# The end of a softmax attention: last scores in five accumulator banks, and the next norm begun ahead of the barrier

## What is computed

```python
def _layernorm(x, axis=-1, eps=1e-05):
    m = jnp.mean(x, axis=axis, keepdims=True)
    v = jnp.var(x, axis=axis, keepdims=True)
    return (x - m) / jnp.sqrt(v + eps)

# layer 1, attention: x is (2, 1024, 128), 16 heads of 8 features
scores = jnp.einsum('bhsd,bhed->bhse', q, k) * scale
attn = jax.nn.softmax(scores, axis=-1)
out = jnp.einsum('bhse,bhed->bhsd', attn, v)
...
return out @ Wo.T + bo          # added to the residual stream

# layer 1, experts: top 1 of 8, x is the normalised residual stream
router_logits = x @ Wr.T
expert_idx = jnp.argmax(jax.nn.softmax(router_logits, axis=-1), axis=-1)
```

## Time and profile before

| | |
|---|---|
| three timed runs | 938.89, 940.71, 941.74 us; median 940.71 |
| profiled execution | 944.2 us, its span 942.9 us |
| busy in the span | TensorE 757.7, VectorE 669.1, ScalarE 509.2, GpSimd 244.2 us |
| attention 1 | about 450 to 820.7 us |
| experts 1 | 820.7 us to the end |

### The profile page before, as it was taken

The page is one execution under the profiler, slowest core; times in us unless marked ns, Lnnn a source line. Parts: engine busy times, 40 slices in busy tenths (PEclk is TensorE's granted clock), DMA queues, the critical chain, the costliest instruction groups (busy, mean ns, idle before and its releaser), DMA issues. The chain is left out here.

```text
span 942.9 us, 17693 instructions
## 1 busy us (share of the span) xinstructions
PE 757.7 (80%) x6704; PEld 324.7 (34%) x6704; DVE 669.1 (71%) x1321; ACT 509.2 (54%) x1003; POOL 244.2 (26%) x297
## 2 busy tenths in 40 slices
PE   6879987976419999937887999999999999628780
PEld 3332245633316676624111222222222222215560
DVE  7879944467673434448786999999999998553545
ACT  4723522555304333343346888888888888404343
POOL 0130010323045666560651200000100000025653
PEclk9989999988659999977658999999999999858996
DMA  3520010000541111131876030321300000051112
GB/s 92 127 54 2 1 24 5 5 1 0 231 158 37 44 43 42 38 100 51 230 158 188 2 80 2 80 47 36 80 2 2 3 2 12 16 235 42 42 34 95
DMA packets 40618, 57.62 MB, mean 61 GB/s; under 512 B 12424, under 2 KB 27920, under 8 KB 39768
## 3 DMA queue, kind: packets, MB, share of 16 engines
q1 hardware_dynamic: 36568, 48.36, 18.9%
q0 software_dynamic: 3968, 8.13, 3.0%
HBM read 37.54 MB, written 14.75 MB: 55 GB/s over the span
## 5 line engine op out<-in xcount | busy, mean ns | idle before, releaser
L983 DVE TENSOR_REDUCE arena<-psum 128x1 f32<-128x1024 f32 x256 | 300.9, 1217 | 23.9 <-PE psum L877 21.2
L1113 ACT ACTIVATE arena<-psum 128x512 f32<-128x512 f32 x512 | 266.8, 604 | 57.2 <-PE psum L894 57.2
L877 PE MATMUL psum<-arena 56*128 56x512 bf16 x512 | 180.8, 413 | 10.9 <-DVE arena L983 9.2
L894 PE MATMUL psum<-arena 59*128 59x512 bf16 x512 | 157.8, 390 | 8.1 <-ACT arena L1113 6.1
L905 PE MATMUL psum<-arena 128*32 128x512 f32 x1024 | 138.1, 611 | 8.7 <-issue 8.7
L894 PEld LDWEIGHTS psum<-arena 59*128 59x128 bf16 x512 | 38.3, 94 | 172.2 <-ACT arena L1113 148.8
L473 POOL DMA_INDIRECT rows_y<-arena x62 | 61.7, 996 | 62.7 <-DVE arena L424 59.7
L381 PEld LDWEIGHTS psum<-arena 128*128 128x128 f32 x496 | 62.3, 191 | 39.2 <-issue 29.7
L381 PE MATMUL psum<-arena 128*128 (+1 forms) x496 | 66.8, 278 | 10.7 <-ACT arena L452 10.4
L372 PE MATMUL psum<-arena 128*128 x124 | 67.5, 627 | 3.0 <-DVE arena L409 2.6
L468 POOL DMA_INDIRECT arena<-rows_x,arena x62 | 60.3, 972 | 35.3 <-issue 16.9
(11 more groups left out here) (305 smaller groups left out, 1111.8 us busy)
## 6 DMA issues: line engine op xcount, KB each, us to landing
arena<-scr_k SPq DMA_DIRECT2D x15, 448.0 KB
arena<-scr_q SPq DMA_DIRECT2D x15, 448.0 KB
arena<-in_f_up SPq DMA_DIRECT2D x1, 4096.0 KB, 13.7
arena<-rows_y SPq DMA_DIRECT2D x12, 256.0 KB, 4.8
scr_q<-arena SPq DMA_DIRECT2D x6, 384.0 KB, 3.7
arena<-in_f_down SPq DMA_DIRECT2D x1, 2048.0 KB, 19.8
rows_x<-xn SPq DMA_DIRECT2D x2, 1024.0 KB, 16.6
arena<-in_f_up SPq DMA_DIRECT2D x1, 2048.0 KB, 8.6
```

What stands on the lines that cost most here:

```text
L877: mm = pe.matmul(ps[:, bank + half, :], q[rows, k, h, (qh * 4 + qt) * P:(qh * 4 + qt + 1) * P], kk[rows, k, h, half * BLK:(half + 1) * BLK ...
L894: pe.matmul(ps[:, n % 3, :], kk[0:KA, k, h, kb * P:(kb + 1) * P], q[0:KA, k, h, qh * BLK:(qh + 1) * BLK], start=True, stop=True).then_inc( ...
L983: dve.tensor_reduce(mx[:, qh, h * 4 + qt:h * 4 + qt + 1], ps[:, bank:bank + 2, :].rearrange("p a b -> p (a b)"), X, ALU.max).then_inc(S("a ...
L1113: act.activation(pt[:, (u % 3) * HG + h, :], ps[:, n % 3, :], ACT.Exp, scale=float(HD) ** -0.5).then_inc(S("a1_exp"), 1)
```

## The change

The edits, by what they do.

1. **Five banks.** From score 464 on (the first of unit 116) the scores go through banks 5, 6 and the three old ones in turn. A score waits for the last exponential that read its bank, and the first in banks 5 and 6 for all 256 row maxima. `project_out(2)` and `project_out(3)`, whose banks are 5 and 6, wait for the last exponential that reads them.
2. **The norm of blocks 0 to 2 ahead of the barrier.** VectorE takes the variance plus epsilon of 12 tiles after `add_out(2)`, their reciprocals and an offset (mean x -1 x reciprocal) after `turn_back(3)`, and the four rows of block 0; ScalarE takes the root and, as one activation each with scale and offset, the eight rows of blocks 1 and 2; TensorE transposes the three blocks behind `project_out(3)`, in banks 0 to 2; ScalarE copies them to `xnT`.
3. **Behind the barrier** only block 3 is left: 4 columns of roots, 4 rows, 4 transposes, one copy. SyncE's `rows_out_sp` of this stage waits for a row count of 8 in place of 16 (the rows that ScalarE makes are not in that count).
4. `retire` leaves the semaphores with `_landed` and `_stored` in their names alone (eight of the `f0_` stage).

```diff
-def rows_out_sp(c, name, k):
-    c.sp.wait_ge(c.sem("n_row"), NT * (c.turn + 1))
+def rows_out_sp(c, name, k, rows=NT):
+    c.sp.wait_ge(c.sem("n_row"), NT * c.turn + rows)
...
-    rows_out_sp(c, "f1", 1)
+    rows_out_sp(c, "f1", 1, 2 * TPB)
...
 def ffn1_dve(c, x):
-    norm_roots(c, 1e-5)
-    for n in range(NB):
-        norm_rows(c, x, n)
+    last = slice(3 * TPB, NT)
+    dve.wait_ge(own.sem, own.n)
+    dve.tensor_scalar(m["rs"][:, last], m["mv"][:, last, 1], 1e-5, None, ALU.add).then_inc(S("n_var"), 1)
+    dve.wait_ge(S("n_root"), c.turn + 1)
+    dve_step(c, dve.reciprocal(m["rs"][:, last], m["rs"][:, last]))
+    norm_rows(c, x, 3)
...
 def ffn1_act(c):
-    norm_act(c, (6, 7), xnt_block(c))
+    act.wait_ge(S("n_var"), c.turn + 1)
+    act.activation(rs[:, 3 * TPB:NT], rs[:, 3 * TPB:NT], ACT.Sqrt).then_inc(S("n_root"), 1)
+    act.wait_ge(S("n_turned"), NB * (c.turn + 1))
+    act.copy(xnt_block(c)(3), c.psum[:, 6, :]).then_inc(S("n_xnt"), 1)
...
 def ffn1_pe(c):
-    norm_pe(c, (6, 7))
+    c.pe.wait_ge(c.sem("n_row"), NT * c.turn + 2 * TPB)
+    for j in range(TPB):
+        mm = c.pe.transpose(c.psum[:, 6, j * P:(j + 1) * P], c.mem["xn"][:, 3 * TPB + j, :], c.mem["ident"][:])
+    mm.then_inc(c.sem("n_turned"), 1)
...
+LAST_MAXIMA = (TILES - AHEAD + 1) // 2 + 1
+def score_bank(n):
+    first = LAST_MAXIMA * HG
+    return n % 3 if n < first else ((5, 6) + tuple((first + k) % 3 for k in range(3)))[(n - first) % 5]
+def score_ahead(n):
+    return max((k for k in range(max(0, n - 5), n) if score_bank(k) == score_bank(n)), default=None)
...
-        if n >= 3:
-            pe.wait_ge(S("a1_exp"), n - 2)
-        pe.matmul(ps[:, n % 3, :], kk[0:KA, k, h, kb * P:(kb + 1) * P],
+        if score_ahead(n) is not None:
+            pe.wait_ge(S("a1_exp"), score_ahead(n) + 1)
+        elif n >= LAST_MAXIMA * HG:
+            pe.wait_ge(S("a1_red"), TILES)
+        pe.matmul(ps[:, score_bank(n), :], kk[0:KA, k, h, kb * P:(kb + 1) * P],
...
     def project_out(b):
         pe.wait_ge(S("a1_back"), b + 1)
+        pe.wait_ge(S("a1_exp"), max((n + 1 for n in range(LAST_MAXIMA * HG, G * U * HG) if score_bank(n) == 3 + b), default=1))
...
     project_out(3)
+    for b in range(3):
+        pe.wait_ge(S("n_row"), NT * (c.turn + 1) + TPB)
+        if b:
+            pe.wait_ge(S("a1_nrow"), TPB * b)
+        for j in range(TPB):
+            mm = pe.transpose(ps[:, b, j * P:(j + 1) * P], c.mem["xn"][:, b * TPB + j, :], m["ident"][:])
+        mm.then_inc(S("n_turned"), 1)
...
     turn_back(2)
     add_out(2)
+    mv, rs, most = c.mem["mv"], c.mem["rs"], slice(0, 3 * TPB)
+    dve.wait_ge(own.sem, own.n)
+    dve.tensor_scalar(rs[:, most], mv[:, most, 1], 1e-5, None, ALU.add).then_inc(S("a1_nvar"), 1)
     turn(halves - 1)
     turn_back(3)
+    dve.wait_ge(S("a1_nroot"), 1)
+    dve_step(c, dve.reciprocal(rs[:, most], rs[:, most]))
+    at = slice(TPB, 3 * TPB)
+    dve.scalar_tensor_tensor(m["a1_off"][:], mv[:, at, 0], -1.0, rs[:, at], ALU.mult, ALU.mult).then_inc(S("a1_noff"), 1)
+    dve.wait_ge(S("a1_back"), 1)
+    norm_rows(c, x, 0)
     add_out(3)
...
     table_ahead(c)
+    rs, xn, most = c.mem["rs"], c.mem["xn"], slice(0, 3 * TPB)
+    act.wait_ge(S("a1_nvar"), 1)
+    act.activation(rs[:, most], rs[:, most], ACT.Sqrt).then_inc(S("a1_nroot"), 1)
+    act.wait_ge(S("a1_back"), 3)
+    act.wait_ge(S("a1_noff"), 1)
+    for t in range(TPB, 3 * TPB):
+        act.activation(xn[:, t, :], x[:, t, :], ACT.Identity, scale=rs[:, t:t + 1],
+                       bias=m["a1_off"][:, t - TPB:t - TPB + 1]).then_inc(S("a1_nrow"), 1)
+    for b in range(3):
+        act.wait_ge(S("n_turned"), NB * (c.turn + 1) + b + 1)
+        act.copy(xnt_block(c)(b), ps[:, b, :]).then_inc(S("n_xnt"), 1)
```

More of the change, by code:

```diff
@@ L84, in retire @@
     def retire(self, prefix):
-        self.cleared = [self.named.pop(n) for n in list(self.named) if n.startswith(prefix)]
+        self.cleared = [self.named.pop(n) for n in list(self.named)
+                        if n.startswith(prefix) and "_landed" not in n and "_stored" not in n]
         for s in self.cleared:
@@ L795, in attn1_memory @@
     c.sb("a1_rd", [P, 2, BLK // 32])
+    c.sb("a1_off", [P, 2 * TPB])
 def attn1_ahead(c):
@@ L1043, in attn1_dve, with attn1_act @@
     add_out(2)
+    mv, rs, most = c.mem["mv"], c.mem["rs"], slice(0, 3 * TPB)
+    dve.wait_ge(own.sem, own.n)
+    dve.tensor_scalar(rs[:, most], mv[:, most, 1], 1e-5, None, ALU.add).then_inc(S("a1_nvar"), 1)
     turn(halves - 1)
     turn_back(3)
+    dve.wait_ge(S("a1_nroot"), 1)
[4 more added lines that the diff above has]
+    norm_rows(c, x, 0)
     add_out(3)
-def attn1_act(c):
+def attn1_act(c, x):
     act, ps, m, S = c.act, c.psum, c.mem, c.sem
@@ L1112, in attn1_act @@
                 act.wait_ge(S("a1_pv"), u - 2)
-            act.activation(pt[:, (u % 3) * HG + h, :], ps[:, n % 3, :], ACT.Exp, scale=float(HD) ** -0.5).then_inc(S("a1_exp"), 1)
+            act.activation(pt[:, (u % 3) * HG + h, :], ps[:, score_bank(n), :], ACT.Exp, scale=float(HD) ** -0.5).then_inc(S("a1_exp"), 1)
         if u == 0:
@@ L1292, in attn1 @@
     attn1_pe(c)
-    attn1_act(c)
+    attn1_act(c, x)
     attn1_dve(c, x)
```

## The result

The changed kernel takes 936.84 us as the median of 20 runs, against 943.72 for the kernel before in 20 runs made beside them: ratio 0.9937 with a 95% interval of 0.992 to 0.9953, which is 4.4 to 7.5 us less. The forecast was 4.9 less. Two later sets of the same kernel gave 0.9957 (0.9942 to 0.9971) and 0.9942 (0.992 to 0.9963). The profiled execution has a span of 936.1 us against 942.9.

The account below looks back on a forecast made before the run. Three banks tie TensorE and ScalarE in the last scores, then a serial chain follows the barrier. Barrier 1.95 us earlier plus 3.2 behind it gives 5.1, cut to 4.9 by the rows' landing: 940.7 - 4.9 = 935.8 us, range 933.4 to 938.7.

Parts of the forecast that it names:

- Banks: Last score units of the attention: five banks remove a 0.42 us stop per period, 4.4 us gained.
- Rival A: Attention's last units: scores do not speed up, gain only 0.5 us (940.2); 10 in 100, including half the banks' gain.
- The tail: End of attention: ScalarE's last copy, at 818.4, holds the barrier, which opens 1.95 us earlier.
- Behind the barrier: Barrier to router logits: only one block's norm is left, 3.2 us gained, 5.1 in all.
- the same again ... 5.1 in all, up to the places: After the last transposes: 3.0 us to the logits as before, the rest unchanged, places at 838.3.
- The rows' transfer: Normalised rows to memory: landing stays 19.8 us behind the barrier's opening, at 838.5, just behind the places.
- the gather starts at 838.5 + 0.8: First gather: starts 0.8 us after the rows' landing, at 839.3, making the sum 4.9 us.
- The loop: Expert loop: same work, costed at nothing; a clock shift of one or two tiles, 1 to 2 us either way.
- rival B: Expert loop: more tiles at half clock, 0.95 us each; slower from eight more, twelve give 947; 4 in 100.
- The total: Whole kernel: 4.9 us gained on the median 940.7, giving 935.8.
- The 1.95 and the 3.2: Forecast gains in us: the barrier opening earlier, and the shorter stretch from there to the logits; 5.1 together.

Follow-up runs that it names:

- e4: The full change plus ten matmuls whose result nobody reads, placed in TensorE's routing waits (1, 5 and 4); ratio to the kernel before 0.9948.
- e8: The full change run again unaltered, in the second set of runs; ratio to the kernel before 0.9957.
- e5: The full change with the three copies to xnT and block 2's transposes back behind the barrier; ratio to the kernel before 0.9943.
- e6: The full change with copies behind the barrier, rows' transfer ahead of the biases, and unread matmuls (1, 8, 4) in the routing; ratio to the kernel before 0.9925.
- e10: The full change run again unaltered, in the third set; 937.74 us, ratio to the kernel before 0.9942.
- e3: The full change with the normalised rows' transfer issued ahead of the 2 MB of biases; ratio to the kernel before 0.9967.
- e11: The kernel before plus the five banks and 13 unread matmuls in the routing, norm behind the barrier as before; ratio to the kernel before 0.9921.
- e9: The kernel before plus the five banks alone, in the third set; 937.97 us, ratio to the kernel before 0.9946.
- e2: The full change with three banks as before, so only the norm part; ratio to the kernel before 1.0017.
- e1: The kernel before plus the five banks alone, in the first set; ratio to the kernel before 0.9976.
- the three together: The full change with copies behind the barrier, rows' transfer ahead of biases, and unread matmuls in the routing; ratios to the kernel before 0.9925 and 0.99.

## Why the prediction was right

**Banks: right.** The stop of 0.42 us in each period went entirely, the period is 1.97 us, and the exponentials are over 4.27 us earlier (4.4 forecast). The rule behind it, that either engine could run at 1.95 to 1.97 once three banks did not tie them, came from the spacing in the earlier trace rows and the issue times in the earlier trace rows. Rival A is out.

**The tail: right.** ScalarE's third copy holds the barrier, which opens 1.86 us earlier (1.95 forecast), and 2.3 when TensorE's clock is still full (e4, e8). VectorE ends 2.2 before it. e5 shows that the copy, and no other thing, held it.

**Behind the barrier: right to the logits, 0.5 us off after them.** The logits came 4.93 us after the opening (4.9). The step that failed is "the same again ... 5.1 in all, up to the places": it took what follows the logits as unchanged. The counts' products ran at half clock and the places gained 4.5. Before (L200, L201), then in the change (L202, L203):

```profile
831.14 0.49 PE L200 MATMUL psum<-arena 128*128 128x128 f32 x2 [2.46 <-DVE arena L241]
831.47 0.39 PE L201 MATMUL psum<-arena 128*128 128x128 f32 x2
```

```profile
822.73 0.80 PE L202 MATMUL psum<-arena 128*128 128x128 f32 x2 [2.46 <-DVE arena L243]
823.32 0.64 PE L203 MATMUL psum<-arena 128*128 128x128 f32 x2
```

The forecast had weighed the clock for the transposes and for the loop, but not for the products between. Where the clock had come back (e5, e6) the places are 19.6 us behind the opening, in the change 20.1.

**The rows' transfer: its landing right in kind and 0.4 us off, its part in the gather wrong.** It landed 20.3 us after the opening and not 19.8, still within a few tenths of the places. But "the gather starts at 838.5 + 0.8" took the step from the places to the gather, 0.8, as the step from the landing. That step was 0.61 here and 0.26 in e4, so the landing held nothing, and in e10, where it came 0.1 ahead of the places, the gather stood at the same 58.2. The row behind the landing is the 16.8 us that the transfer took from its issue, which was 1.6 us earlier relative to the barrier. With the places late, and the gather 0.8 behind them, the sum at the gather is 4.5 us, in all three traces of the change between 4.5 and 5.0, against 4.9. The Trainium skill's statement ("DMA: Bandwidth & Descriptors", on two DMAs through the same engine) that one queue's descriptors start in order agrees with e3, which shows landings and not starts: issued ahead of the 2 MB, the rows land 4.6 us earlier and the biases last.

**The loop: inside the range.** In the first trace of the change the loop took 1.1 us more than before, of which 0.85 is one more tile at half clock, the small form of rival B; in e10 it took 0.5 more, with the traces of the faster set not comparable. Rival B itself, eight tiles more, was not seen in the three traces of the change. The Trainium skill ("TensorE: Matmul & The Clock Gate", the HAM clock gate) says that idle time throttles the array and that the release varies; the traces agree: the fall came ahead of `project_out(3)` in e11 and behind it in e9, and the same 16 transposes took 3.77 us in e9, the clock coming back at their end, and 4.19 in the kernel before.

**The total: partly luck.** The forecast of 4.9 lies within the measured 4.4 to 7.5, but it reached the gather with 0.4 us too much and put the loop at nothing, where the traces of the change lose 0.5 to 1.1 against the one trace before. What is left, 3.4 to 4.0 us, lies just below the interval of the first timed runs (4.4 to 7.5) and within those of the two later sets (2.7 to 5.4 and 3.5 to 7.5). Whatever more the first runs gained has no place in these traces.

**What the prediction did not work out** is the case that mattered most for understanding the change: the banks alone. Its own terms would have given it, 4.4 us at the barrier and the same 4.4 at the gather. The 1.95 and the 3.2 that it adds look like gains of the norm part, but 1.95 is 4.3 from the banks less 2.4 that the norm part costs, so that the norm part is worth 3.2 - 2.4 = 0.8 at the places, and 0.3 once the counts' products run at half clock (e2). Beside the banks its worth goes by the clock: in e1 and e9, where the clock came back early, the places of the banks alone are 0.9 us ahead of the change's; in e11, where it did not, 1.2 behind. A sum over a change with two parts should be made for each part alone.

## What to carry to other kernels

Two engines that hand buffers round in a ring can both show idle time and both be called the bound; work out each one's period alone, and if both are shorter than the period seen, more buffers give the difference, here 0.42 us in each of 11 periods. Moving work in front of a barrier pays only what is not added to the engine that arrives last: move what the barrier's followers need first (the rows), and leave behind it what hides there (the copies). And look what else is tied to the barrier's opening: the transfers issued behind it kept their distance to it here (landing 19.8 to 20.3 us after it in every run with the old order of issue), whatever the chain beside them gained. And when a profile names the event that came last, compare the step from it with the same step in other runs before calling it the cause.

## What the runs showed that was not expected

TensorE's granted clock links places far apart. With 16 transposes in a row behind the barrier it came back to 1.0 for the router's products in two traces (e1, e9: 1.17 us for 32 of them) and not in two others (before and e11: 1.93 and 1.94), but in all four for the counts' products (in e11 an unread matmul stood between). With four transposes there, in e2, e3 and the three traces of the change, both ran at half clock, and in the first trace of the change it stayed at 0.50 until the experts' loop. In the loop each tile at 0.50 costs about 0.95 us. Matmuls that nobody reads cost 0.89 us each at full clock (4.46 for five) and 1.6 at half (6.52 for four): where they were meant to hold the clock and came too late, they held up the real work by 1.1 us.

Between sets of runs the stretch from the first gather to the end differs by 12.5 to 13.5 us for one program (99.2 and 86.7 us for the change, 98.5 and 85.1 for the three together), although the record gives the same chip, 7, for both. The traces of the slower sets have two to four waits of 1.4 to 3.4 us in the chain of the loop that are put down to "another core or an unknown queue", and those of the faster have none. What these are stays open; the kernel before has them too, so it is not the change.
